# Cross-attention and fp4 feed-forward on one core: key and query split, parts of the maxima, fp4 scaling and up product moved to GpSimd

## What is computed

```python
x = x + xattn(layernorm(x), ctx, Wq, Wk, Wv, Wo, bo)     # x (16, 512, 256), ctx (16, 1601, 192)
x = x + ffn(layernorm(x), w_gate, w_up, w_down)
# xattn: 16 heads of 16; softmax(Q K^T * 0.25) V, then @ Wo + bo
# ffn:   h = silu(fp4(x) @ fp4(w_gate)^T) * (fp4(x) @ fp4(w_up)^T); fp4(h) @ fp4(w_down)^T   (704 hidden)
# fp4:   per block of 16 values scale = max|x| / 6; x / scale is rounded to a grid of eight magnitudes, then * scale
```

## Time and profile before

| what | value |
|---|---|
| time, median of 3 runs | 3927.74 us (3926.81 to 3930.73) |
| span of the profiled execution, first to last instruction | 3925.2 us |
| mean granted TensorE clock, share of full speed | 0.983 |
| time per entry, in the middle of the program | about 238 us |
| events that move, in half steps | 22, 48, 74, 100 (maxima); 38, 74 to 95 (projections) |

### The profile page before, as it was taken

The page is one execution under the profiler, slowest core; times in us unless marked ns, Lnnn a source line. Parts: engine busy times, 40 slices in busy tenths (PEclk is TensorE's granted clock), DMA queues, the critical chain, the costliest instruction groups (busy, mean ns, idle before and its releaser), DMA issues.

```text
span 3925.2 us, 73982 instructions
## 1 busy us (share of the span) xinstructions
PE 3745.4 (95%) x19654; PEld 1618.5 (41%) x19654; DVE 2997.8 (76%) x6641; ACT 2260.4 (58%) x4414; POOL 870.2 (22%) x917
## 2 busy tenths in 40 slices
PE   7999999999999999999999999999999999999997
PEld 2324444344443444434444344443434434344434
DVE  6787787787877877777877777877788777878774
ACT  2656565555655556555565556656565565655562
POOL 2221212222112211222212122221222111222113
PEclk8999999999999999999999999999999999999998
DMA  2222121121211122121121211212111211211100
GB/s 64 50 48 54 22 57 34 33 51 34 50 33 42 39 42 49 26 48 36 39 55 23 53 34 34 53 34 47 36 39 41 43 46 29 45 38 39 37 22 7
DMA packets 148169, 157.83 MB, mean 40 GB/s; under 512 B 58129, under 2 KB 118818, under 8 KB 147746
## 3 DMA queue, kind: packets, MB, share of 16 engines
q1 hardware_dynamic: 147746, 152.78, 17.8%
HBM read 39.53 MB, written 8.39 MB: 12 GB/s over the span
## 4 chain that ended last, share of the span: by engine, by line
PE 78%; DVE 11%; issue 4%; ACT 4%; SPq 1%; DMA 1%; DVEq 0%; POOL 0%; ACTq 0%
PE out_ps L815 17%; PE score_ps L804 16%; PE piece_ps L829 16%; PE work L769 8%; PE work L780 5%; DVE piece_max L1096 4%; PE work L744 3%; ACT probs L913 3%; PE work L737 3%; PE work L743 2%; PE work L735 2%; PE work L722 1%; PE work L759 1%; PE work L753 1%; PE work L727 1%
## 5 line engine op out<-in xcount | busy, mean ns | idle before, releaser
L1096 DVE TENSOR_REDUCE piece_max<-piece_ps 128x1 f32<-128x400 f32 (+1 forms) x4096 | 2144.8, 568 | 680.1 <-PE piece_ps L829 665.2
L913 ACT ACTIVATE probs<-score_ps 128x512 f32<-128x512 f32 (+1 forms) x3328 | 1876.8, 597 | 1085.1 <-PE score_ps L804 1061.0
L829 PE MATMUL piece_ps<-k_stack,q_stack 96*128 96x400 bf16 (+1 forms) x4096 | 1294.0, 339 | 55.5 <-DVE piece_max L1096 51.1
L804 PE MATMUL score_ps<-q_stack,k_stack 99*128 99x512 bf16 (+1 forms) x3328 | 1269.1, 388 | 67.6 <-issue 20.9
L815 PE MATMUL out_ps<-probs,v_ones 128*17 128x512 f32 x6656 | 886.9, 605 | 2.1 <-ACT probs L913 0.9
L804 PEld LDWEIGHTS score_ps<-q_stack,k_stack 99*128 99x128 bf16 (+1 forms) x3328 | 326.1, 99 | 910.1 <-ACT probs L913 639.0
L829 PEld LDWEIGHTS piece_ps<-k_stack,q_stack 96*128 96x128 bf16 x4096 | 389.7, 98 | 700.5 <-DVE piece_max L1096 484.4
L1148 POOL TENSOR_TENSOR h<-h,h_grid 128x704 f32<-128x704 f32 (+1 forms) x68 | 111.2, 1636 | 1106.5 <-DVE h_grid L965 1106.5
L769 PE MATMUL work<-wgu_T,xq_T 128*128 128x256 f32 (+1 forms) x1440 | 345.8, 362 | 0.4 <-ACT xq_T L887 0.4
L769 PEld LDWEIGHTS work<-wgu_T,xq_T 128*128 128x128 f32 x1440 | 258.7, 189 | 49.0 <-ACT xq_T L887 3.4
L815 PEld LDWEIGHTS out_ps<-probs,v_ones 128*17 128x17 f32 x6656 | 110.6, 95 | 277.5 <-issue 233.3
(11 more groups left out here) (142 smaller groups left out, 2846.0 us busy)
## 6 DMA issues: line engine op xcount, KB each, us to landing
k_stack<-k_parts SPq DMA_DIRECT2D x1536, 50.0 KB, 2.2
q_stack<-q_parts SPq DMA_DIRECT2D x1536, 16.0 KB, 1.8
ctx_in<-in_ctx SPq DMA_DIRECT2D x48, 384.0 KB, 3.4
x_in<-in_x SPq DMA_DIRECT2D x16, 512.0 KB, 3.7
resid<-in_x SPq DMA_DIRECT2D x16, 512.0 KB, 3.7
out<-y SPq DMA_DIRECT2D x64, 128.0 KB, 1.9
q_stack<-neg_rows SPq DMA_DIRECT2D x192, 4.0 KB, 1.7
ctx_in<-in_ctx SPq DMA_DIRECT2D x16, 48.8 KB
```

The source lines that it names most:

```text
L804: pe.matmul(score_ps[0:r, n % SCORE_RING, :], k_stack[:, par, slot(g, j), m * P:m * P + r], q_stack[:, par, slot(g, j), :], start=True, st ...
L829: pe.matmul(piece_ps[:, n % PIECE_RING, 0:hi - lo], q_stack[0:SROWS, par, slot(g, j), t * P:(t + 1) * P], k_stack[0:SROWS, par, slot(g, j) ...
L913: act.activation(probs[0:r, step % 2, j, :], score_ps[0:r, (PER_GROUP * m + j) % SCORE_RING, :], ACT.Exp, scale=SCORE_SCALE).then_inc(prob ...
L1096: dve.tensor_reduce(piece_max[:, row, c:c + 1], piece_ps[:, n % PIECE_RING, 0:piece_at[c + 1] - piece_at[c]], AX_X, ALU.max).then_inc(piec ...
```

## The change

- **Split.** ACT copies the round as it is (f32) into `raw`, which takes the place of `rest`, and thereby empties the bank. POOL makes all three parts: part 0, the difference in place in `raw`, part 1, part 2. A split is now four instructions on POOL. DVE has no share in it. ACT's copy number n waits until split n-2 is complete, since `raw` has two halves.
- **Maxima.** DVE keeps the reduction (1009); its four instructions that make the parts are done by POOL.
- **fp4 scaling.** The product with the inverse scale moves from DVE to POOL, placed at `ln2_apply`, `h_scale` and `w_scale`; DVE's grid instructions wait for it.
- **Up product.** ACT makes 0.5 * up into `up_half` ahead of the tanh; DVE's first instruction now empties the bank; POOL multiplies the two into `h`. ACT's event j waits for POOL's product j-2, and `h_max` waits for the third product.
- **Output.** `down` is added into x1 in place and stored from there; `y` is gone, and `out_proj` waits for the store of the entry before.
- **Start.** The five memsets of ones in `k_stack` stand ahead of DVE's first event instead of between the prologue's projections.

No table changes: PE has the same matmuls in the same order.

```diff
+        raw = sb("raw", [P, 2, NQ], F32)
...
-        y = sb("y", [P, 2, D], F32)
+        up_half = sb("up_half", [P, 2, GW], F32)
...
-                elif name == "q_proj":
-                    act.copy(q_parts[:, event[1], 0, :], work[:]).then_inc(part0_ready, 1)
-                elif name == "k_proj":
-                    e, c = event[1:]
-                    a, w = chunk(c)
-                    act.copy(k_parts[:, e, 0, a:a + w], work[:, 0:w]).then_inc(part0_ready, 1)
+                elif name in ("q_proj", "k_proj"):
+                    n = split_number(kind, event)
+                    w = NQ if name == "q_proj" else chunk(event[2])[1]
+                    if not (kind == "start" and n < 2):
+                        act.wait_ge(split_step, count(nxt, SPLITS * 2 * (CHUNKS + 1), SPLITS * (n - 1)))
+                    act.copy(raw[:, n % 2, 0:w], work[:, 0:w]).then_inc(this_drained, 1)
...
-                        act.wait_ge(silu_step, count(old, n * QT, n * t + j))
+                        act.wait_ge(h_ready, count(old, n * QT, n * t + j - 1))
+                    act.mul(up_half[:, (n * t + j) % 2, 0:w], work[:, GW:GW + w], 0.5)
...
-                elif name in ("q_proj", "k_proj"):
-                    half = event[1]
-                    if name == "q_proj":
-                        n, a, w, parts = split_number(kind, event), 0, NQ, q_parts
-                    else:
-                        n, (a, w), parts = split_number(kind, event), chunk(event[2]), k_parts
-                    dve.wait_ge(part0_ready, count(nxt, 2 * (CHUNKS + 1), n + 1))
-                    if not (kind == "start" and n < 2):
-                        dve.wait_ge(split_step, count(nxt, 4 * (CHUNKS + 1), 2 * n - 2))
-                    dve.tensor_tensor(rest[:, n % 2, 0:w], work[:, 0:w], parts[:, half, 0, a:a + w],
-                                      ALU.subtract).then_inc(this_drained, 1)
...
+                    if g or not at_start(of):
+                        dve.wait_ge(shift_step, step(0))
                     dve.tensor_reduce(neg_max[:], piece_max[:], AX_X, ALU.max, negate=True).then_inc(shift_step, 1)
-                    dve.wait_ge(shift_step, step(1))
-                    dve.tensor_copy(neg_parts[:, 0, :], neg_max[:]).then_inc(shift_step, 1)
-                    dve.wait_ge(shift_step, step(2))
-                    dve.tensor_tensor(neg_rest[:], neg_max[:], neg_parts[:, 0, :], ALU.subtract).then_inc(shift_step, 1)
-                    dve.wait_ge(shift_step, step(3))
-                    dve.tensor_copy(neg_parts[:, 1, :], neg_rest[:]).then_inc(shift_step, 1)
-                    dve.wait_ge(shift_step, step(4))
-                    dve.tensor_tensor(neg_parts[:, 2, :], neg_rest[:], neg_parts[:, 1, :], ALU.subtract).then_inc(shift_step, 1)
...
+                    dve.wait_ge(x1_free[t % 2], count(old, 32, 16 * (t // 2 + 1)))
...
-                                             op0=ALU.add, op1=ALU.mult).then_inc(silu_step, 1)
-                    dve.wait_ge(silu_step, count(old, n * QT, n * t + j + 1))
-                    dve.scalar_tensor_tensor(out=q.h[:, j * GW:j * GW + w], in0=tanh_g[:, half, 0:w], scalar=0.5,
-                                             in1=work[:, GW:GW + w], op0=ALU.mult, op1=ALU.mult).then_inc(this_drained, 1)
-                elif name in ("h_max", "h_scale", "h_grid"):
+                                             op0=ALU.add, op1=ALU.mult).then_inc(this_drained, 1)
...
-                    dve.wait_ge(y_free[t % 2], count(old, 32, 16 * (t // 2 + 1)))
-                    dve.tensor_tensor(y[:, t % 2, :], work[:, 0:D], x1[:, t, :], ALU.add).then_inc(this_drained, 1)
+                    dve.tensor_tensor(x1[:, t, :], work[:, 0:D], x1[:, t, :], ALU.add).then_inc(this_drained, 1)
...
+            for n in range(PER_GROUP + 1):
+                dve.memset(k_stack[SROWS:SROWS + SHIFT, :, n, :], 1.0).then_inc(cleared, 1)
...
+            def fp4_scale(src, inverse, ready, total):
+
+                pool.wait_ge(ready, total)
+                pool.tensor_tensor(fp4_blocks(src), fp4_blocks(src), over_block(inverse, src.shape[1] // BLOCK), ALU.mult).then_inc(ready, 1)
...
+                    of = raw[:, n % 2, 0:w]
+                    step = (lambda k: count(nxt, SPLITS * 2 * (CHUNKS + 1), SPLITS * n + k))
+                    pool.tensor_tensor(parts[:, half, 0, a:a + w], of, zero[:].broadcast_to([P, w]), ALU.add).then_inc(split_step, 1)
+                    pool.wait_ge(split_step, step(1))
+                    pool.tensor_tensor(of, of, parts[:, half, 0, a:a + w], ALU.subtract).then_inc(split_step, 1)
+                    pool.wait_ge(split_step, step(2))
+                    pool.tensor_tensor(parts[:, half, 1, a:a + w], of, zero[:].broadcast_to([P, w]), ALU.add).then_inc(split_step, 1)
+                    pool.wait_ge(split_step, step(3))
+                    pool.tensor_tensor(parts[:, half, 2, a:a + w], of, parts[:, half, 1, a:a + w],
                                        ALU.subtract).then_inc(split_step, 1)
+                elif name == "max_parts":
+                    g = event[1]
+                    step = (lambda k: count(nxt if g == 0 else batch, 5 * PHASES, 5 * g + k))
+                    none = zero[:].broadcast_to([P, PER_GROUP * QT])
+                    pool.wait_ge(cleared, 2)
+                    pool.wait_ge(shift_step, step(1))
+                    pool.tensor_tensor(neg_parts[:, 0, :], neg_max[:], none, ALU.add).then_inc(shift_step, 1)
+                    pool.wait_ge(shift_step, step(2))
+                    pool.tensor_tensor(neg_rest[:], neg_max[:], neg_parts[:, 0, :], ALU.subtract).then_inc(shift_step, 1)
+                    pool.wait_ge(shift_step, step(3))
+                    pool.tensor_tensor(neg_parts[:, 1, :], neg_rest[:], none, ALU.add).then_inc(shift_step, 1)
+                    pool.wait_ge(shift_step, step(4))
+                    pool.tensor_tensor(neg_parts[:, 2, :], neg_rest[:], neg_parts[:, 1, :], ALU.subtract).then_inc(shift_step, 1)
...
+                elif name == "ln2_apply":
+                    fp4_scale(q.xq, q.xq_small[:, 2, :], xq_step, count(old, 7 * QT, 7 * event[1] + 4))
+                elif name == "gate_up":
+                    t, j = event[1:]
+                    w, n = gate_w[j], len(gate_w)
+                    pool.wait_ge(*drained(kind, batch, event))
+                    pool.tensor_tensor(q.h[:, j * GW:j * GW + w], tanh_g[:, (n * t + j) % 2, 0:w], up_half[:, (n * t + j) % 2, 0:w],
+                                       ALU.mult).then_inc(h_ready, 1)
+                elif name == "h_scale":
+                    fp4_scale(q.h, q.h_small[:, 2, :], h_step, count(old, 7 * QT, 7 * event[1] + 4))
```

More of the change, by code:

```diff
@@ L43 @@
 SHIFT = 3
+SPLITS = 4
 TINY = 1e-12
@@ L466, in build @@
         h_round = sem("h_round")
+        h_ready = sem("h_ready")
         w_step = sem("w_step")
@@ L481, in build @@
         shift_loaded = [sem(f"shift_loaded{i}") for i in range(2)]
-        y_free = [sem(f"y_free{i}") for i in range(2)]
+        x1_free = [sem(f"x1_free{i}") for i in range(2)]
         KSTACKED = 16 * len(STACK)
@@ L506, in quarter @@
             old_v = v_ones[:, B % 2].rearrange("p m h v -> p (m h v)")
-            old_rest = rest[:].rearrange("p s q -> p (s q)")
+            old_raw = raw[:].rearrange("p s q -> p (s q)")
             small, big = 3 * D // BLOCK, 3 * F // BLOCK
@@ L512, in quarter @@
                 xq=x_in[:, t, :], xq_grid=x_T[:, t // 2, t % 2 * D:(t % 2 + 1) * D],
-                xq_small=flat(old_rest, t * small, 3, D // BLOCK), h_small=flat(old_rest, QT * small + t * big, 3, F // BLOCK),
+                xq_small=flat(old_raw, t * small, 3, D // BLOCK), h_small=flat(old_raw, QT * small + t * big, 3, F // BLOCK),
                 h=flat(old_v, t * F, F), h_grid=flat(old_probs, t * F, F),
@@ L953, in fp4_max @@
                 dve.tensor_scalar(inv, amax, BELOW_TIE, None, ALU.mult).then_inc(done, 1)
-            def fp4_scale(src, small, done, base):
-                dve.wait_ge(done, base(4))
-                n = src.shape[1] // BLOCK
-                dve.tensor_tensor(fp4_blocks(src), fp4_blocks(src), over_block(small[:, 2, :], n), ALU.mult).then_inc(done, 1)
             def fp4_grid(src, grid, done, base):
@@ L1081, in handle @@
                         fp4_max(src, small, w_step, base)
-                    elif name == "w_scale":
-                        fp4_scale(src, small, w_step, base)
                     else:
@@ L1114, in body @@
                         handle(kind, batch, drain)
-                        if kind == "start" and drain[:2] in (("k_proj", 0), ("q_proj", 0)):
-                            write_ones(split_number(kind, drain))
                         drain = None
@@ L1158, in handle @@
                 name = event[0]
-                if name in ("out_proj", "xq_scale", "h_grid"):
+                if name in ("out_proj", "ln2_apply", "xq_scale", "gate_up", "h_scale", "h_grid"):
```

(6 more changed lines are left out.)

29 lines of the change are left out of this document (9 added, 20 removed).

## The result

The changed kernel took **4061.35 us** (median of 4 runs, 4045.61 to 4070.48), the kernel before 3927.27 us in the runs beside it (3925.82 to 3930.73). The ratio is 1.0338 (95% interval 1.0322 to 1.0355): 134 us slower, where the forecast was 82. The time is inside the range (3955 to 4090), in its upper half. The profiled execution of the changed kernel took 4045.61 us (span 4043.8), so that the two traces are compared over 4043.8 - 3925.2 = 118.6 us, 15 less than the medians.

What follows compares the result with a forecast made beforehand. The kernel was taken as bound by PE for most steps, with DVE pacing a few places. Terms A to H summed to +82 us on a 3925.2 us span, 4007; the median 2.5 above, 4010 us; range 3955 to 4090.

Steps and rivals of the forecast that it cites:

- C: Half step 82: DVE's two grid instructions wait for running POOL split instructions, 0.5 us x 15 = +7 us (0 to 22).
- A: Half step 38: POOL's 4.6 us splits delay ACT's copies and an exponential; PE loses 2.6 us x 15 = +39 us.
- B: Half steps 74 to 79: maxima's parts and layer norm's root late on POOL, +1.0 us x 15 = +15 us.
- D: Half step 23: first group's maxima parts later behind half-product, product and slower tiny instructions, +0.8 us x 16 = +12 us.
- E: Half step 48: maxima find POOL idle, only 0.3 us for hops, x 16 = +5 us (0 to 6).
- F: Half steps 91 to 93: DVE, the pacer, loses its 0.88 us scaling, -0.6 us x 15 = -9 us.
- H: Tail: POOL's rounding ahead of the next quarter's products, slower scaling and product, +6 us (2 to 9).
- Half step 100: Maxima at half step 100: PE comes to them later than they are ready, so nothing.
- G: Start: five memsets ahead of the statistics, then POOL's splits, delay the first group's loads, +7 us (5 to 8).
- Rival 1: DVE's relief counts, POOL's queue does not; A, B and C vanish, gain 49 us: 3879 us, chance 0.10.
- Rival 2: Moves cancel within 0.2%: PE has more work ahead of each wait than seen; 3928 us, chance 0.04.
- Rival 3: POOL's queue grows: whole 4.4 us in A, double waits in B and C; +159, 4087 us, chance 0.18.

Runs made afterwards that it cites:

- eight and ten copies: Kernel before, ACT held ahead of the fifth cast of half step 38 by copies to a scratch tile: eight 3955.68 us, ten 4000.15 us.
- the two runs on the split: Changed kernel with the split of keys and queries as before: 3945.89 us; kernel before with only the split moved to POOL: 4006.75 us.
- the split alone: Kernel before with only the split moved to POOL, behind ACT's raw copies: 4006.75 us.
- the new order: Changed kernel, fifth copy's own place, memsets behind layer norm, POOL's root ahead of second query split and scaling ahead of key split: 3933.62 us.
- the fifth copy's own place: Changed kernel with 66 more columns in `raw`, so the fifth copy waits only for the split five before it: 3986.56 us.

## Why the prediction was right, and where it was not

Its sign and its places stood, all but C, and so did the queue and the waits behind A; the total was 52 us short, within its bounds. Between the two traces the terms sum to 117 us, 35 over the forecast's 82; the other 17 lie between these traces and the medians, and no trace shows where.

- **A** was mis-sized: "PE loses 2.6 us, since it has some work ahead of that score" (39 us), measured 77. The chain of copies, splits and waits came out as worked: splits of 4.5 (4.6), waits of the fifth copy 3.9 (4), PE's wait 2.23 (2.6). What failed is the step from PE's wait to time lost. It took the engine behind the wait to be as fast as ahead of it. The run with useless matmuls shows the missing 2.7 us per entry as half clock, 40 us in all, which is more than the 35 of the traces; the other terms nearly cancel. The eight and ten copies show some 1.9 us for it, in a kernel without POOL's share. That the range held the time is in part luck: its upper bound took "the whole 4.4" here, which was a bound for another reason, the lateness of the exponentials.
- **B**: forecast 15, measured 26. The parts came later by 0.79 us (0.9 forecast) and the root at the time given, one slot behind the split. Half step 78 lost the 1.0 us that was forecast, but by luck: the late root left only some 0.2 of it, and some 0.7 came from the normalization, whose meeting with a POOL instruction the prediction hadn't seen. In 5 of the 14 entries half clock follows, 1.7 us each, 8 us in all. That two moves were needed together for the second half was in the prediction's chain, but not said, and my expectations for the two runs on the split missed for it.
- **C** came to nothing, though one of the two grid instructions does take 1.13 instead of 0.29 us in every middle entry. The relief from the subtraction alone doesn't hide that: half step 82 loses 0.54 us with the split alone, where DVE still does the scaling, and 0.25 with the new order. Why it is hidden in the changed kernel wasn't tested. **D** was 5 instead of 12: the 0.8 us added ACT's half-product and POOL's product in full, and the run with the product put back shows them as nothing; only the four instructions count. **E** (3 of 5), **F** (-6 of -9) and **H** (5 of 6) are right; of H, 2.6 us are the product. **Half step 100**, costed at nothing, lost 0.34 us, which is gone with the parts back on DVE: PE does come there before the parts are ready.
- **G** was 14 instead of 7: the memsets have 0.62 us between them, so the statistics began at 18.9, not 16.0; and the term followed POOL's chain of splits alone, where PE was late too, waiting 9.4 us for its input and then at half clock. Without the split on POOL the first score is still at 98.6 us. The loads did wait for POOL as forecast, but the longer splits by themselves are 3.3 us. The start differs between traces for other reasons too (94.1 us with the scaling alone, 110.2 and 118.8 us in the two with long half clock), so that its size is good to some us only.
- Not forecast: the gain of 7 us in the first entry beside A; 4.5 us of it are there with the scaling alone, where POOL scales the weights.

Rival 1 (DVE's relief counts) is refuted as a whole: 264 us off DVE gave only F and half step 76 here (and 0.65 us at half step 78 in runs where the root isn't late). Rival 2 (moves cancel, 3928 us) is refuted by the time. Rival 3 (4087 us) came near the time for a wrong reason, POOL's queue; the fifth copy's own place left that queue as it was and took 75 us away. What stays open is where the 17 us between the traces' sum and the medians lie, since only one run of each kernel has a trace.

## What to carry to other kernels

Price a new wait of the matmul engine as the wait plus what the clock takes afterwards; here a hold that was 1.05 us longer cost 3.0 us more. When work moves to an idle engine, its share of busy time says little: look for the in-order engine that must wait for it, count how many buffers lie between them, and ask what stands behind the waiting instruction. Here 66 columns of buffer, and the order of two items in POOL's queue, were worth 75 and 38 us of a change that had cost 134.

## What the runs showed of the hardware

- After waits of PE of 2.23 us (changed kernel) and 1.53 us (ten copies) the granted clock fell to 0.50 for 3.4 to 10.2 us, in 14 and 12 of the 14 middle entries; after one of 0.48 us it stayed at 1.00 in 13. After the same wait of 2.24 us (split alone) it stayed in 2 of 14. Filling the wait with useless matmuls kept it at 1.00 in all 15.
- The half clock at half step 40 cost 2.7 us per entry.
- A DVE instruction of 16 columns with two SBUF inputs took 0.96 instead of 0.17 us when a POOL instruction of 512 columns had started 0.1 us ahead of it; the normalization (256 columns) took 1.12 instead of 0.40 us when one had started 0.07 us ahead.
- A memset of 3 partitions x 3204 columns takes 2.73 us, and 0.62 us passes before the next.
